# The end of a cross-attention stage: the output product of the last pair but one split by sequence and head, one product of the next group's recurrence moved behind it, and the closing norm done half by half

## The reference, cut to what matters

```
x = _layernorm(x + _L0_attn_ref(x, ...))        # recurrence (RWKV)
x = _layernorm(x + _L0_xattn_ref(x, ctx, ...))
x = _layernorm(x + _L0_ffn_ref(x, ...))         # experts, top 1
x = _layernorm(x + _L1_attn_ref(x, ...))
x = _layernorm(x + _L1_xattn_ref(x, ctx, ctx, ...))   # this change
x = _layernorm(x + _L1_ffn_ref(x, ...))         # experts, top 2
```

```
Q, K, V = _proj(x, Wq, bq), _proj(ctx, Wk, bk), _proj(ctx, Wv, bv)
scores  = einsum('bhqd,bhkd->bhqk', Q, K) / sqrt(64)
context = einsum('bhqk,bhkd->bhqd', softmax(scores), V)
return einsum('bse,de->bsd', context (heads side by side), Wo)
```

## Time and profile before

| what | value |
|---|---|
| median of 3 runs | 1147.87 us (1147.84 to 1147.91) |
| the profiled execution | 1145.93 us, its span 1144.0 us |
| mean granted TensorE clock | 0.999 of full speed |
| busy: TensorE (PE), its weight loads (PEld) | 93%, 59% of the span |
| busy: VectorE (DVE), ScalarE (ACT), GpSimd (POOL) | 63%, 56%, 15% |

### The profile page before, as it was taken

One profiled execution on the slowest core, in us unless ns is written; L12 is line 12 of the kernel. 1 busy time (PEld: TensorE's weight loads), 2 busy tenths in 40 slices (PEclk: granted clock), 3 DMA queues, 4 the chain that ended last, 5 costly groups with the idle time before them and its releaser, 6 DMA issues.

```text
span 1144.0 us, 23634 instructions
## 1 busy us (share of the span) xinstructions
PE 1068.9 (93%) x9157; PEld 677.0 (59%) x9157; DVE 722.5 (63%) x1837; ACT 645.0 (56%) x1428; POOL 167.1 (15%) x237
## 2 busy tenths in 40 slices
PE   8889999999989998999898999999999999999997
PEld 6663564556775455555686455555577636645576
DVE  6542676888643376788854248688884417678871
ACT  5560457775644165777556236677656505577724
POOL 3310400122020030021102012020212004000000
PEclk9999999999999999999999999999999999999999
DMA  8400000000000000000000000000000000000000
GB/s 254 126 1 1 1 2 11 2 19 2 1 11 1 1 1 2 10 20 2 2 2 11 1 1 1 4 9 20 2 1 10 1 1 1 2 1 2 2 2 10
DMA packets 21074, 15.81 MB, mean 14 GB/s; under 512 B 871, under 2 KB 18644, under 8 KB 20956
## 3 DMA queue, kind: packets, MB, share of 16 engines
q1 hardware_dynamic: 20932, 14.24, 4.1%
q10 hardware_dynamic: 24, 0.01, 0.0%
HBM read 13.18 MB, written 1.05 MB: 12 GB/s over the span
## 4 chain that ended last, share of the span: by engine, by line
PE 66%; issue 12%; ACT 9%; DVE 8%; DVEq 2%; POOL 1%; SPq 1%; POOLq 1%; DMA 0%; ACTq 0%
PE ps L768 10%; PE ps L962 7%; PE ps L998 7%; PE ps L980 5%; PE ps L800 4%; PE ps L806 3%; PE ps L797 3%; ACT arena L1436 2%; PE ps L1007 2%; PE ps L900 2%; ACT arena L1200 2%; PE ps L1135 2%; PE ps L1126 2%; PE ps L858 1%; PE ps L871 1%
## 5 line engine op out<-in xcount | busy, mean ns | idle before, releaser
L1200 ACT ACTIVATE arena<-ps 128x512 f32<-128x512 f32 (+6 forms) x300 | 162.6, 574 | 120.8 <-PE ps L980 56.2
L2131 DVE TENSOR_REDUCE nmax<-ps 128x1 f32<-128x512 f32 x256 | 163.8, 682 | 23.8 <-PE ps L962 23.2
L1436 ACT ACTIVATE arena<-ps,nmax 128x512 f32<-128x512 f32 x256 | 173.4, 684 | 8.0 <-DVE nmax L2131 4.8
L1608 POOL TENSOR_TENSOR rstd<-mv,neg_half 128x2 f32<-128x2 f32 x72 | 49.8, 691 | 721.1 <-DVE mv L1779 721.0
L2136 DVE COPY arena<-ps 128x512 f32<-128x512 f32 x128 | 88.1, 688 | 60.9 <-PE ps L980 60.9
L980 PEld LDWEIGHTS ps<-ident,arena 64*128 64x128 f32 x2048 | 76.4, 138 | 82.6 <-issue 42.3
L768 PE MATMUL ps<-big,w1a 128*128 128x512 f32 x256 | 117.3, 604 | 0.0
L980 PE MATMUL ps<-ident,arena 64*128 64x64 f32 x2048 | 92.2, 228 | 11.7 <-ACT arena L1200 6.2
L768 PEld LDWEIGHTS ps<-big,w1a 128*128 128x128 f32 x256 | 46.3, 189 | 57.5 <-issue 56.5
L2023 DVE TENSOR_TENSOR big<-XT,ps 128x512 f32<-128x512 f32 x32 | 22.0, 687 | 90.4 <-PE ps L752 90.3
L1362 ACT ACTIVATE big<-ps 128x512 f32<-128x512 f32 x16 | 9.6, 597 | 116.1 <-PE ps L768 116.1
(11 more groups left out here) (388 smaller groups left out, 1996.0 us busy)
## 6 DMA issues: line engine op xcount, KB each, us to landing
ctx<-in_ctx_dram SPq DMA_DIRECT2D x4, 512.0 KB, 4.2
w1a<-in_L_ffn_W_dram SPq DMA_DIRECT2D x1, 2048.0 KB, 9.3
w1b<-in_L_ffn_W_dram SPq DMA_DIRECT2D x1, 2048.0 KB, 11.2
w2b<-in_L_ffn_W_dram SPq DMA_DIRECT2D x8, 256.0 KB, 5.3
X<-in_x_dram SPq DMA_DIRECT2D x4, 256.0 KB, 2.9
out_dram<-Y SPq DMA_DIRECT2D x4, 256.0 KB, 2.3
arena<-in_L_xattn_Wq_dram SPq DMA_DIRECT2D x1, 512.0 KB
arena<-in_L_xattn_Wk_dram SPq DMA_DIRECT2D x1, 512.0 KB
```

The lines of the kernel that those rows point to most:

```text
L1200: return act.activation(dst, src, ACT.Copy)
L1436: act.activation(cprob[:, 2 * (t % 2) + h, :], bank(2 * (t % 2) + h), ACT.Exp, bias=nmax[:, s:s + 1], accum_out=rsum[:, j % 2, s:s + 1]).t ...
L2131: dve.tensor_reduce(nmax[:, s:s + 1], bank(s % 4), AX.X, ALU.max, negate=True)\
```

## The change

- `project_out_by_head(6, 0, 7)`: the first sequence of pair 6 is multiplied already at tile 3 of pair 6, into bank 7 alone. Both heads lie in the one bank, so the second head waits for the first (`head_ps`). In groups 0 to 2 this takes the place of `rec_project(it + 1, 2, 7)`.
- The product beside tile 2 of pair 7 is that of the second sequence alone.
- VectorE adds the first head of it (`add_early`, 2 instructions) ahead of `turned(7, 0)`, the second head behind it; of the second sequence it adds the first head between `turned(7, 2)` and `turned(7, 3)` and the second head after `turned(7, 3)`.
- At the end each half is added, measured and normalised before the next half is begun.
- TensorE turns the first half as soon as it is normalised, then makes `rec_project` (groups 0 to 2), then 14 filling transposes (22 in the last group) in place of 34 and 4.

```diff
+                def project_out_by_head(j, seq, b):
+                    pe.wait_ge(context_ready, it * (PAIRS * GROUP) + j * GROUP + seq + 1)
+                    for h in range(2):
+                        if h:
+                            pe.wait_ge(head_ps, it + 1)
+                        r = slice(h * DK, (h + 1) * DK)
+                        for t in range(seq * QT, (seq + 1) * QT):
+                            o = (h * QT + t % QT) * D
+                            last = pe.matmul(ps[:, b, o:o + D], CTs[r, j % 2, t * P:(t + 1) * P],
+                                             xwT[r, 3, j, :], start=True, stop=True)
+                        last.then_inc(wo_ps if h else head_ps, 1)
...
                     if t == 2 and j == PAIRS - 1:
-                        project_out(j - 1, range(GROUP), 0)
+                        project_out(j - 1, [1], 0)
...
-                    if t == 3 and j == 6 and more_groups:
-                        queries_read(7)
-                        rec_project(it + 1, 2, 7)
+                    if t == 3 and j == PAIRS - 2:
+                        queries_read(PAIRS - 1)
+                        project_out_by_head(j, 0, 7)
...
                 project_out(PAIRS - 1, [1], 4)
-                keep_awake(6, 34)
+                turn_x(it, 5, [0])
+                if more_groups:
+                    pe.wait_ge(wo_added, (it + 1) * (PAIRS - 1))
+                    rec_project(it + 1, 2, 7)
+                keep_awake(6, 14 if more_groups else 22)
...
-                turn_x(it, 5, between=4)
+                turn_x(it, 5, [1])
                 keep_awake(6, 3)
...
+                def add_early(j, h, b):
+                    if h == 0:
+                        dve.wait_ge(wo_ps, it * (PAIRS + 2) + j + 1)
+                    for t in tiles_of(0):
+                        o = (h * QT + t % QT) * D
+                        dve.scalar_tensor_tensor(out=X1[:, t, :], in0=ps[:, b, o:o + D],
+                                                 scalar=cross_inv[:, j % 2, 2 * t + h:2 * t + h + 1], in1=X1[:, t, :],
+                                                 op0=ALU.mult, op1=ALU.add)
...
                 def pair(j):
+                    last_pair = j == PAIRS - 1
+                    if last_pair:
+                        add_early(j - 1, 0, 7)
                     turned(j, 0)
+                    if last_pair:
+                        dve.drain()
+                        add_early(j - 1, 1, 7)
                     row_max_ahead(j, 0, 0)
...
                     row_max_ahead(j, 2, 0)
+                    if last_pair:
+                        dve.wait_ge(wo_ps, it * (PAIRS + 2) + j + 1)
+                        add_products(j - 1, 0, tiles_of(1), 0)
                     turned(j, 3)
...
-                    if j:
-                        add_pair(j - 1, 4 if j < PAIRS - 1 else 0)
+                    if last_pair:
+                        dve.drain()
+                        add_products(j - 1, 1, tiles_of(1), 1).then_inc(wo_added, 1)
+                    elif j:
+                        add_pair(j - 1, 4)
...
                 for seq in range(GROUP):
                     add_last(seq)
                     moments(X1, seq).then_inc(var_ready, 1)
-                for seq in range(GROUP):
                     dve.wait_ge(rstd_ready, it * (LNS * GROUP) + 4 * GROUP + seq + 1)
                     normalised(X1, X, seq).then_inc(layer_done, 1)
```

More of the change, by code:

```diff
@@ L360, in decoder_kernel @@
         wo_ps, wo_added = semaphore("wo_ps"), semaphore("wo_added")
+        head_ps = semaphore("head_ps")
         r1_ps, e1_arg, e1_exp = semaphore("r1_ps"), semaphore("e1_arg"), semaphore("e1_exp")
@@ L495, in turn, with turn_x @@
                 return last
-            def turn_x(it, n, between=0):
-                for seq in range(GROUP):
-                    if seq:
-                        keep_awake(6, between)
+            def turn_x(it, n, seqs=range(GROUP)):
+                for seq in seqs:
                     pe.wait_ge(layer_done, it * (LAYERS * GROUP) + (n - 1) * GROUP + seq + 1)
@@ L2143, in add_products @@
                     return last
+                def add_early(j, h, b):
[6 more added lines that the diff above has]
+                                                 op0=ALU.mult, op1=ALU.add)
                 def add_pair(j, b):
-                    dve.wait_ge(wo_ps, it * (PAIRS + 1) + j + 1)
+                    dve.wait_ge(wo_ps, it * (PAIRS + 2) + j + 1)
                     add_products(j, 0, range(TT), b)
@@ L2203, in add_last @@
                 def add_last(seq):
-                    dve.wait_ge(wo_ps, it * (PAIRS + 1) + PAIRS + seq)
+                    dve.wait_ge(wo_ps, it * (PAIRS + 2) + PAIRS + 1 + seq)
                     for h in range(2):
```

## The result

The changed kernel takes 1149.98 us (median of 20 runs, 1148.32 to 1151.24), the kernel before 1147.57 us (median of 20, 1145.92 to 1149.52). The ratio is 1.0024, 95% interval 1.0018 to 1.0030: 2.4 us slower, just over the 0.2% that the prediction had named as the edge of no change. It forecast 1149.3 with 1147.0 to 1151.3, so the time is in the range, and the side was named right as a small loss. Of the prediction's own three cases the ratio picks "slower by over 0.2%", which had a chance of 0.20. The time itself, 1149.98, is under the 1150.2 that was the edge of that case, because the kernel before now has a median of 1147.57 in place of 1147.87.

What follows compares the result with a forecast made beforehand. VectorE's list bounds the stage's end; in pair 7 the bound passes between VectorE and TensorE. Per group -1.51 + 0.43 + 1.43 = +0.35 us, four groups 1.4, added to 1147.87: 1149.3 us, range 1147.0 to 1151.3.

Steps and rivals of the forecast that it cites:

- slower by over 0.2%: Whole kernel: the case of a time over 1150.2 us, chance 0.20.
- Two additions at tile 0: VectorE, pair 7, behind the copy of tile 0: the row maximum and everything behind come later, +0.43 us per group.
- The half by half norm: Closing norm on VectorE: wait for the root and first normalisation stand ahead of the second half, 0.35 + 1.08 = +1.43 us.
- the first half's earlier time is worth nothing: End of the stage: the stage ends when the second half is normalised; the first half's own time matters to nobody.
- the halved product beside tile 2: TensorE, pair 7: worth nothing, since the turn after it waits for the copy of tile 2 anyway.
- additions in idle time: VectorE, pair 7, between the copies of tiles 2 and 3: 0.56 us in 0.85 of idle time, price 0.
- price nothing: TensorE, pair 6's early product: lasts 0.85 us (0.7 to 1.2), costs nothing; at the upper end 0.17 in the last group.
- Rival B: TensorE behind its last product: granted clock falls in each group, time outside 1147.0 to 1151.3; chance 0.04.
- Rival D: Early product doesn't stay hidden: head wait, early additions, new order cost 0.6 us or more per group, 1150.3 to 1151.5; chance 0.13.
- Rival A: Pair 7: the delay is absorbed and the tail's sequence alone counts, -0.08 us per group, 1147.5; chance 0.12.
- Rival C: Cast of the expert indices: its collision with GpSimd's multiplication goes away in three groups, 2.4 us gained, 1146.9; chance 0.05.

## Why the prediction was right, and where it was not

The mechanism held: the early additions shorten VectorE's tail, two of them delay tile 0, and the norm done half by half puts a wait for GpSimd and a normalisation ahead of the second half. In group 2 the path from pair 5's product to the second normalisation grew in three parts:

| part | forecast | measured |
|---|---|---|
| pair 5's product to the copy of tile 0 | 0 | +0.12 (4.94 against 4.82) |
| copy of tile 0 to the copy of tile 3 | +0.43 | +0.35 (6.99 against 6.64) |
| copy of tile 3 to the second normalisation | -0.08 | -0.06 (8.18 against 8.24) |
| sum | +0.35 | +0.41 |

Two additions at tile 0 are on the path: shown, since moving them off gives 0.27 back and puts the row maximum back. They delay the row maximum by the 0.43 of the forecast, but the copy of tile 1 follows it 0.59 us later in place of 0.66, so less arrives. This partly offset the early product's 0.12, which is luck. The half by half norm, +1.43 per group: +1.46 measured alone, with its two waits of 0.81 us where 0.7 to 0.8 were forecast. That the first half's earlier time is worth nothing is shown by the same run. That the halved product beside tile 2 and the additions in idle time cost and give nothing: their idle time is there, 0.33 us left of 0.85.

The early product "price nothing" was the first term mis-sized. Its length, put at 0.85 us with 1.2 as the upper end, was 1.30: each head alone takes about as long (0.66 and 0.64 from its start to the next start) as both together unsplit, and the trace has the second head's weight loads too starting only after the wait; the 0.25 us of idle time is only part of that. It put +0.1 us per group on the path, which making the heads apart took off again. With it the order costs 0.41 in group 2 (20.11 - 19.70), 0.39 and 0.38 in groups 0 and 1 and 0.36 in the last (19.87 - 19.51): 1.5 us, forecast 1.4.

Rival B, given 0.04 as a fall in each group, happened in a smaller form: in group 0 of the profiled execution, 0.83 us. What the prediction read from its rows, that 1.05 us of idle time did no harm, is right as far as it goes; it had said itself that no row is as long as 1.3, and weighed that too lightly. Sum: 1.54 + 0.83 = 2.4, the measured difference of the medians. That the fall occurs in most of the 20 runs is inferred, not seen in their traces: from this sum, from the lowest runs (1148.32 against 1147.66 with the idle time filled), and from the mean granted clocks of the runs in the lower cluster (0.996 or 0.997 in eight of the changed kernel's ten, 0.998 or 0.999 in all five with the idle time filled). So a third of the 2.4 us came from a mechanism that only rival B named, at 0.04 and as a fall in every group. The range took it in because its upper part had been left open for other things, which is luck too.

The base of the forecast was a little high, too. The three runs that gave 1147.87 all lay in the upper cluster, and the profiled execution in the lower; the 20 runs have 1147.57. Counted from there the forecast of +1.4 would have been 1149.0. Rival D's "0.6 us or more per group" (1150.3) overlapped with the forecast's own upper bound of 0.65 (1150.5), so their chances weren't cleanly apart.

By the Trainium skill (TensorE: Matmul & The Clock Gate, section on what's actually happening) the throttled state is the default and activity releases it. The traces agree in so far as the grant fell at two of four ends where filling alone had been removed; they don't make it certain, since the two ends of 1.49 us kept the 2.4 GHz level.

Rival A, the delay absorbed: out, the values of the first sequence start behind a wait of 0.27 us for VectorE's copy. Rival C: out, the cast of the expert indices keeps 0.96 to 1.00 us in three groups and 0.17 in the last. Rival D in part: the early product went over its upper end.

## What to carry to other kernels

Two halves in one engine's list, each with a round trip to another engine, should be written as work, work, result, result: the second half's work covers the first's wait, and finishing the first half sooner is worth only what somebody does with it. Before an operation is split to fill idle time, ask whether the idle time lies before or behind the instruction that the other engine waits for; here the same two additions cost 0.36 us in front of it and 0.10 behind. A change of two parts can hide a gain in a larger loss: here some 3 us gained by one part and about 5 lost by the other came out as a loss of 0.2%, so time the parts singly. And where runs of one kernel lie in two clusters, compare the same stretch of two traces before trusting the medians of a few runs.

## What the runs showed of the hardware that was not expected

The granted clock fell to its 1.2 GHz level for a few microseconds behind idle times of 1.39, 1.42 and 1.50 us (0.50 from 1110 to 1115 us with less filling), and did not behind others of 1.30, 1.39 and 1.49 us, nor behind 0.84 and 1.05. Such a fall cost 0.83 us in one place, 2.8 in another and 0.1 in a third. At the program's start, with a clock of 0.66 from 25 to 30 us, 14 transposes took 3.25 us in place of 1.75, and pair 5's product of group 0 stood 1.75 us late, more than the 1.5 us that the new order itself costs. A TensorE instruction that waited for the engine's own last result cost 0.25 us of idle time, and the eight matmul records around it took 1.30 us in place of 0.65.
